# Copying the gather indices once per window of eight chunks, in a graph attention kernel

## The chip, the cores and the metric

The kernel runs on one core of a Trainium2 chip. The metric is the device time of one execution in microseconds; of several executions the median is given.

## What is computed

The reference is a pre-norm residual layer around one graph attention layer, with N = 6250 nodes, D = 256 features and E = 200000 edges. The edges are sorted by their destination node `dst`; the sources `src` are random. Cut to what matters:

```python
h = relu(layernorm(x))
q, k, v = h @ wq + bq, h @ wk + bk, h @ wv + bv
scores = sum(q[dst] * k[src], -1) * D ** -0.5 + (edge_weight * we + be)
exp_s = exp(scores - segment_max(scores, dst)[dst])
attn = exp_s / max(segment_sum(exp_s, dst)[dst], 1e-12)
out = segment_sum(v[src] * attn[:, None], dst)
y = layer_norm(h + out + h @ ws + bs, g1, b1)
z = layer_norm(y + gelu(y @ w_ff1 + b_ff1) @ w_ff2 + b_ff2, g2, b2)
return x + z
```

The destinations are drawn as N times the square of a uniform number, so low node numbers have more edges than high ones.

## The kernel before

The program has three blocks, one after the other. The first makes h for 49 blocks of 128 nodes, stores h in HBM (`h_rows`), folds the query and key weights into one projection that is kept in SBUF in three bf16 parts (`q3`), and prepares tables. The second, the edge block, goes over all edges. The third divides the sums by the weights, applies the value projection, and does the feed forward part and both norms.

The edge block, on which the change bears, cuts the sorted edges into **chunks** of 512 edges (C = 512, J = 4 columns of 128). There are 391 chunks, padded to TP = 392. G = 8 chunks make a **window** (line 25 gives G, and NW = 49 windows). A **step** is one pair of a chunk and a block of 128 destination nodes: a chunk whose edges cross from one node block into the next takes two steps, which is why there are more steps than chunks. A table, `steps_tab`, gives each step its chunk and block. The engines do the following:

- **POOL** (line 776 on, helper `gather`) fetches the source rows. For each chunk it waits until the chunk's slot in `rows` is free (semaphore `slot_free`) and until the indices are there (`idx_set`). Then come four times an indirect DMA of 128 rows of 1 KB from `h_rows` (line 787), and behind each a copy of one column of indices from the large table `idx_all` to the small tile `idx` (line 789). That column belongs to the chunk four further on (LEAD = 4), so `idx` is a ring of eight chunks by four columns that is always filled half a ring ahead.
- **SP** (lines 753 to 771) waits, chunk by chunk in order, until the four gathers of the chunk have landed (line 756) and raises `chunk_landed` (line 757). Then it waits until the step that used a slot is summed and raises `slot_free`. A gather may be at most LEAD chunks ahead of the last landed one, and eight slots ahead of the last summed one. SP also loads the destinations, half a window at a time (line 770).
- **DVE** per step: the masked maximum (line 971), the dot products of query rows and gathered rows, four of them (line 914, which waits for `chunk_landed`), the sum with the edge term (line 920), the kept maximum (line 976), the one-hot mark of the destinations for a later step (line 903), and the addition into `acc` (line 931). At every eighth step it loads a new piece of the step table.
- **ACT** per step: two exponentials (lines 876 and 877), two copies from PSUM (line 880), and the mask (line 865).
- **PE** per step: transposes (lines 842 and 815), the expansion of the query rows by the one-hot matrix (line 809), and the weighted sum of the gathered rows (line 855).

The first 16 columns of `idx` are set by POOL in the first block (line 369), after `idx_all` is complete.

Of the kernel before, what the change touches and what calls it, by code (L numbers as in the profile page):

```python
# [7 lines left out]
I32 = mybir.dt.int32  # L8
# [5 lines left out]
P = 128  # L14
J = 4
# [4 lines left out]
G = 8  # L20
WC = G // 2
LEAD = 4
# [7 lines left out]
def ceil_div(a, b):  # L30
    return -(-a // b)


def gnn_layer(nc, x, src, dst, edge_weight, wq, bq, wk, bk, wv, bv, ws, bs, we, be, g1, b1, g2, b2,
              w_ff1, b_ff1, w_ff2, b_ff2, out):
    N, D = x.shape
# [7 lines left out]
    B = ceil_div(N, P)  # L44
    NB = B + 1
    T = ceil_div(E, C)
    TP = ceil_div(T, G) * G
    NW = TP // G
# [18 lines left out]
    with ctx:  # L67
        def sb(name, shape, dt=F32):
            return ctx.enter_context(nc.sbuf_tensor(name, shape, dt))

        def sem(name):
            return ctx.enter_context(nc.semaphore(name))

        def dram(name, shape, dt=F32):
            return nc.dram_tensor(name, shape, dt).ap()

        h_rows = dram("h_rows", (B * P, D))
# [26 lines left out]
        free_tab = sb("free_tab", [1, TP + LEAD], I32)  # L104
        idx_all = sb("idx_all", [P, R], I32)
        ew_all = sb("ew_all", [P, R + J])
        idx = sb("idx", [P, G * J], I32)
        dst_words = sb("dst_words", [P, G * C // 2], I32)
        dst_of = dst_words[:].bitcast(I16)
        w1_sb = dst_words[:, 0:DC * F].bitcast(F32).rearrange("p (c n) -> p c n", c=DC)  # L110
# [7 lines left out]
        def part(n, dt=F32):  # L118
            used[0] += n
            assert used[0] <= WORK, used  # L120
            a = work[:, used[0] - n:used[0]]
            return a if dt == F32 else a.bitcast(dt)
# [36 lines left out]
        def spare(n, dt=F32):  # L159
# [18 lines left out]
        at = B * WORDS_B - staged  # L178
# [24 lines left out]
        plan_consts, dst_cast, dst_out, falls_done, ends_compared, chunks_counted, steps_known, sums_known, marked, counts_ready, rows_copied, free_ready, plan_done = (  # L203
            sem(n) for n in ("plan_consts", "dst_cast", "dst_out", "falls_done", "ends_compared", "chunks_counted", "steps_known", "sums_known", "marked",
                             "counts_ready", "rows_copied", "free_ready", "plan_done"))
        plan = sem("plan")
        idx_set, dst_in = sem("idx_set"), sem("dst_in")
# [55 lines left out]
        with nc.Block() as block:  # L263
# [49 lines left out]
            @block.gpsimd  # L313
            def _(pool):
                g = nc.gpsimd
                pool.memset(ident[:], 0.0).then_inc(ident_set, 1)
                pool.wait_ge(ident_set, 1)
                pool.affine_select(out=ident[:], in_=ident[:], compare_op=ALU.not_equal, fill=1.0, base=0,
                                   pattern=[[-1, P]], channel_multiplier=1).then_inc(ident_set, 1)
                pool.iota(row_i, [[1, HEAD]], base=0, channel_multiplier=0)  # L320
                pool.iota(below_i, [[0, 1]], base=0, channel_multiplier=P)
                pool.iota(below_row_i, [[P, P]], base=0, channel_multiplier=0)
                pool.memset(tri, 1.0)
                pool.memset(is_block, 1.0)
                pool.iota(node_i, [[P, NB]], base=0, channel_multiplier=1).then_inc(consts, 1)
                pool.memset(q3[:, B], 0.0)

                pool.wait_ge(x_zero, 1)
                link = 0
                for n, row, parts in ((D, row_of["bs"], s_bias3), (D1, q_bias, q_bias3)):  # L330
                    if n == D:
                        pool.wait_ge(biases_in, 3 * 16)
                    else:
                        pool.wait_ge(wqk_copied, DC + 1)
                    hi, mid, rest = bias_hi[:, 0:n], bias_mid[:, 0:n], bias_rest[:, 0:n]
                    g.tensor_copy(hi, row).then_inc(bias_link, 1)
                    pool.wait_ge(bias_link, link + 1)
                    g.tensor_tensor(rest, row, hi, ALU.subtract).then_inc(bias_link, 1)
                    pool.wait_ge(bias_link, link + 2)
                    g.tensor_copy(mid, rest)  # L340
                    g.tensor_copy(parts[0:1, 0:n], hi[0:1, :]).then_inc(bias_link, 1)
                    pool.wait_ge(bias_link, link + 3)
                    g.tensor_copy(parts[32:33, 0:n], mid[32:33, :])
                    g.tensor_tensor(parts[64:65, 0:n], rest[64:65, :], mid[64:65, :], ALU.subtract).then_inc(bias_link, 1)
                    link += 4
                    pool.wait_ge(bias_link, link)
                g.tensor_copy(onesb_rows, ones[:]).then_inc(biases_split, 1)

                pool.wait_ge(consts, 1)
                g.tensor_copy(srow, row_i)  # L350
                g.tensor_copy(node[:], node_i)
                pool.affine_select(out=tri, in_=tri, compare_op=ALU.is_ge, fill=0.0, base=0, pattern=[[1, P]], channel_multiplier=-1)
                pool.affine_select(out=is_block, in_=is_block, compare_op=ALU.is_ge, fill=0.0, base=B - 1, pattern=[[0, 1]], channel_multiplier=-1)
                g.tensor_copy(below_row, below_row_i)
                pool.memset(pad_s, PAD_DST)
                pool.wait_ge(ends_in, 2 * TG * 16)
                g.tensor_copy(ends, ends_i)
                g.tensor_copy(firsts, firsts_i).then_inc(plan_consts, 1)
                pool.wait_ge(list_in, 3 * 16)
                g.tensor_copy(dst_s[0:EDGE_P, :], dst_a[0:EDGE_P, :]).then_inc(dst_cast, 1)  # L360
                pool.wait_ge(plan_consts, 1)
                g.tensor_scalar(firsts, firsts, -float(P), None, ALU.add).then_inc(plan_consts, 1)
                pool.wait_ge(plan_consts, 2)
                for k in range(TG):
                    g.tensor_scalar(chunk_below[:, k, :], below_row, ends[:, k:k + 1], None, ALU.is_gt)
                    last = g.tensor_scalar(chunk_begun[:, k, :], below_row, firsts[:, k:k + 1], None, ALU.is_gt)
                last.then_inc(ends_compared, 1)
                pool.wait_ge(tab_copied, 2)
                g.tensor_copy(idx[:, 0:LEAD * J], idx_all[:, 0:LEAD * J]).then_inc(idx_set, LEAD)

                def clear(first, end):
                    pool.wait_ge(h_done, min(end, B))
                    pool.memset(acc[:, first:end, :], 0.0)

                for k in range(4):
                    clear(k * XG, (k + 1) * XG)
                clear(FULL, NB)
# [312 lines left out]
        rows = part(S * J * D1).rearrange("p (u j n) -> p u j n", u=S, j=J)  # L690
# [13 lines left out]
        rows_in = [[sem(f"rows_in{u}_{j}") for j in range(J)] for u in range(S)]  # L704
        slot_free, chunk_landed = sem("slot_free"), sem("chunk_landed")
# [4 lines left out]
        with nc.Block() as block:  # L710
# [65 lines left out]
            @block.gpsimd  # L776
            def _(pool):
                n, m, rounds = counts(pool)

                def gather(first, u, next_first):  # L780
                    chunk = pool.to_reg(first + (u + 1))
                    pool.wait_ge(dst_out, 2 * 16)
                    pool.wait_ge(slot_free, chunk)
                    pool.wait_ge(dst_out, 2 * 16)
                    pool.wait_ge(idx_set, chunk)
                    for j in range(J):
                        pool.indirect_dma_start(rows[:, u, j, 0:D], None, h_rows, bass.IndirectOffsetOnAxis(idx[:, u * J + j:u * J + j + 1], 0)).then_inc(rows_in[u][j], 16)  # L787
                        at = (u + LEAD) % G * J + j
                        copied = nc.gpsimd.tensor_copy(idx[:, at:at + 1], idx_all[:, next_first(j)])  # L789
                    copied.then_inc(idx_set, 1)  # L790

                with pool.Fori(0, rounds) as r:
                    with pool.Fori(0, NW - 1) as i:
                        first = pool.snap(pool.to_reg(r * TP + i * G), min_val=0, max_val=B * TP)
                        for u in range(G):
                            gather(first, u, lambda j: bass.ds(i * (G * J) + ((u + LEAD) * J + j), 1))
                    first = pool.snap(pool.to_reg(r * TP + (NW - 1) * G), min_val=0, max_val=B * TP)
                    for u in range(G):
                        gather(first, u, lambda j: slice((((NW - 1) * G + u + LEAD) % TP) * J + j, (((NW - 1) * G + u + LEAD) % TP) * J + j + 1))

            @block.tensor
            def _(pe):
# [587 lines left out]
```

## Time and profile before

| | us |
|---|---|
| median of 3 runs | 2562.84 |
| lowest, highest | 2562.78, 2564.1 |
| profiled execution, own time | 2571.49 |
| profiled execution, span | 2569.4 |

| engine | busy us | share of the span |
|---|---|---|
| PE matmul | 2285.8 | 89% |
| PE weight load | 1811.4 | 70% |
| POOL | 1963.4 | 76% |
| DVE | 1757.6 | 68% |
| ACT | 1141.8 | 44% |

The gathers of the edge block start between 167.3 us and 2251.3 us of the span, so this block is four fifths of the program. The span runs from the first to the last instruction; the execution's own time also has what lies around that. Busy times of different engines overlap. "PEld" in a row is the weight load of PE. A row names the line of the source, the engine, the operation and the tiles it writes and reads; `work` is the large tile that holds `rows` and most of the working buffers, so a gather reads "work<-h_rows,idx". "idle before" is the time for which an engine stood still before an instruction, and the arrow names what ended it; "issue" means that no other engine or transfer did.

### The profile page before, as it was taken

Reading aid. Unit: us, or ns where it says so; the run is one execution under the profiler, and the core shown is the slowest. Engines: PE = TensorE matmul, PEld = TensorE weight load, DVE = VectorE, ACT = ScalarE, POOL = GpSimd, SP = SyncE. Lnnn points to the kernel's source line nnn. Section 1 sums busy time; section 2 is a strip of 40 time slices with the busy share of each in tenths; the row PEclk is TensorE's granted clock in tenths of the full one; section 3 lists DMA queues with packets and bytes.
Section 4 is the critical chain, followed back from the end, with each engine's and each line's share of the span. In section 5 each row is a group of like instructions: output and inputs, shape, how many; then the busy total and the mean of one; then the engine's idle time right before and its main releaser. Section 6 shows DMA issues by size and latency. Waiting matters only on the chain. (4 is left out here: it accounts for less than half of the span.)

```text
span 2569.4 us, 72091 instructions
## 1 busy us (share of the span) xinstructions
PE 2285.8 (89%) x14569; PEld 1811.4 (70%) x14570; DVE 1757.6 (68%) x7421; ACT 1141.8 (44%) x2765; POOL 1963.4 (76%) x3334
## 2 busy tenths in 40 slices
PE   5978888888888889889999999999999999989994
PEld 3756666666666667667677777777777777877883
DVE  5856666666666667667676777777777777775367
ACT  2544333434444444444444444444444444455454
POOL 2148888888888888888888888888888888802355
PEclk7989999999999999999999999999999999999997
DMA  6344444444444444444444444444444444440014
GB/s 201 109 132 123 123 123 122 123 124 123 123 124 123 123 123 124 125 125 124 124 123 124 122 123 124 122 123 124 122 123 124 123 122 123 123 106 29 0 53 138
DMA packets 140341, 302.96 MB, mean 118 GB/s; under 512 B 33710, under 2 KB 76833, under 8 KB 140312
## 3 DMA queue, kind: packets, MB, share of 16 engines
q0 software_dynamic: 75264, 205.62, 28.0%
q1 hardware_dynamic: 62910, 96.62, 11.2%
q10 hardware_dynamic: 2138, 0.40, 0.1%
q8 instruction: 10, 0.16, 0.0%
q14 instruction: 19, 0.16, 0.0%
HBM read 282.87 MB, written 19.65 MB: 118 GB/s over the span
## 5 line engine op out<-in xcount | busy, mean ns | idle before, releaser
L787 POOL DMA_INDIRECT work<-h_rows,idx x1568 | 1527.9, 974 | 252.2 <-issue 252.2
L855 PE MATMUL bank<-work 128*128 x3520 | 837.0, 380 | 0.0
L809 PE MATMUL bank<-q,onehot 128*128 x5304 | 745.4, 275 | 99.9 <-DVE work L914 90.0
L914 DVE SCALAR_TENSOR_TENSOR work<-bank,work 128x257 bf16<-128x257 f32 x1764 | 646.2, 424 | 255.1 <-SPq L757 250.6
L855 PEld LDWEIGHTS bank<-work 128*128 128x128 f32 x3520 | 635.1, 190 | 79.1
L809 PEld LDWEIGHTS bank<-q,onehot 128*128 128x128 bf16 x5304 | 501.4, 98 | 211.2 <-issue 145.3
L876 ACT ACTIVATE work<-work 128x1 f32<-128x1 f32 x440 | 129.6, 295 | 948.7 <-DVE work L971 948.7
L880 ACT COPY work<-bank 128x256 f32<-128x256 f32 x880 | 284.6, 375 | 234.6 <-PE bank L842 233.0
L842 PE MATMUL bank<-ident,work 128*128 128x128 f32 x1760 | 286.5, 285 | 76.9 <-ACT work L877 69.0
L903 DVE TENSOR_SCALAR onehot<-dst_words,node 128x512 bf16 x443 | 168.8, 381 | 263.0 <-issue 211.2
L842 PEld LDWEIGHTS bank<-ident,work 128*128 128x128 f32 x1760 | 184.6, 140 | 232.4 <-ACT work L877 225.3
L971 DVE CUSTOM_DVE_ANT_0 work<-bank,work 128x512 f32<-128x512 f32 x440 | 327.7, 745 | 22.7 <-issue 22.0
L789 POOL COPY idx<-idx_all 128x1 int32 (+1 forms) x1568 | 305.4, 195 | 10.6
L877 ACT ACTIVATE work<-work 128x512 f32<-128x512 f32 x440 | 310.7, 706 | 0.0
L815 PE MATMUL bank<-ident,work 128*128 128x128 f32 x1764 | 275.8, 279 | 26.2 <-DVE work L920 5.0
L865 ACT ACTIVATE work<-onehot 128x512 bf16<-128x512 bf16 x442 | 283.9, 642 | 1.6 <-DVE onehot L903 1.6
L815 PEld LDWEIGHTS bank<-ident,work 128*128 128x128 f32 x1764 | 193.6, 136 | 91.2 <-issue 75.4
L931 DVE SCALAR_TENSOR_TENSOR acc<-acc,work,bank 128x257 f32 x441 | 212.3, 481 | 26.2 <-issue 6.5
L914 DVE DVE_READ_ACCUMULATOR work<-bank,work 128x1 f32 x1764 | 145.1, 82 | 0.0
L920 DVE TENSOR_TENSOR work<-work,ew_all 128x4 f32<-128x4 f32 x441 | 72.3, 164 | 65.6 <-DVE work L914 11.8
L1166 POOL TENSOR_TENSOR work<-work 128x256 f32<-128x256 f32 x49 | 35.8, 730 | 90.2 <-DVE acc L1249 88.2
L1341 PE MATMUL bank<-work,dst_words 128*128 128x128 f32 x784 | 97.7, 278 | 2.7 <-DVE work L1243 2.6
(182 smaller groups left out, 1511.1 us busy)
## 6 DMA issues: line engine op xcount, KB each, us to landing
dst_words<-dst_short SPq DMA_DIRECT2D x99, 512.0 KB
work<-h_rows,idx POOLq DMA_INDIRECT x1568
h_rows<-work SPq DMA_DIRECT2D x49, 128.0 KB, 1.7
r_rows<-work SPq DMA_DIRECT2D x49, 128.0 KB, 1.7
work<-r_rows SPq DMA_DIRECT2D x49, 128.0 KB, 2.1
acc<-in_x SPq DMA_DIRECT2D x4, 1536.0 KB, 15.6
work<-in_x SPq DMA_DIRECT2D x48, 128.0 KB, 2.2
out<-work SPq DMA_DIRECT2D x48, 128.0 KB, 1.9
```

The source lines that it names most:

```text
L787: pool.indirect_dma_start(rows[:, u, j, 0:D], None, h_rows, bass.IndirectOffsetOnAxis(idx[:, u * J + j:u * J + j + 1], 0)).then_inc(rows_i ...
L789: copied = nc.gpsimd.tensor_copy(idx[:, at:at + 1], idx_all[:, next_first(j)])
L809: last = nc.tensor.matmul(banks[j][:, 0:D1], onehot[:, k, j, :], q3[:, bass.ds(b, 1), c, 0:D1], start=(c == 0), stop=(c == 2))
L815: last = nc.tensor.transpose(banks[4][:, j * P:(j + 1) * P], score[:, k, j:j + 1].broadcast_to([P, P]), ident[:])
L842: last = nc.tensor.transpose(banks[5 - half][:, j * P:(j + 1) * P], probsT[:, (2 * half + j) * P:(2 * half + j + 1) * P], ident[:])
L855: last = nc.tensor.matmul(banks[6 + k][:, 0:D1], probs[:, j, :], rows[:, bass.ds(slot, 1), j, :], start=(j == 2), stop=(j == 1))
L865: nc.scalar.activation(outside[:, k, :], onehot[:, k].rearrange("p j n -> p (j n)"), ACT.Copy, scale=BIG, bias=-BIG).then_inc(outside_done, 1)
L877: nc.scalar.activation(probsT, masked, ACT.Exp, bias=new_max, scale=-1.0).then_inc(exp_done, 1)
L880: nc.scalar.copy(probs[:, 2 * half:2 * half + 2, :].rearrange("p j n -> p (j n)"), banks[5 - half][:, 0:2 * P]).then_inc(probs_done, 1)
L914: last = nc.vector.scalar_tensor_tensor(out=product[:, j, 0:D1], in0=banks[j][:, 0:D1], scalar=SCALE, in1=rows[:, bass.ds(slot, 1), j, :], ...
L931: nc.vector.scalar_tensor_tensor(out=a, in0=a, scalar=decay[:, k:k + 1], in1=banks[6 + k][:, 0:D1], op0=ALU.mult, op1=ALU.add).then_inc(ad ...
L971: nc.vector.tensor_tensor_reduce(out=masked, in0=banks[4][:], in1=outside[:, k, :], scale=-1.0, scalar=old_max[:, k:k + 1], op0=ALU.add, o ...
```

## The change

The tile `idx` gets two halves of 32 columns, each of which holds the indices of a whole window. POOL no longer copies a column behind each gather. It issues the four gathers of a chunk one behind another, and behind the gathers of the seventh chunk of a window it copies all 32 columns of the next window into the other half with one instruction. The wait for `idx_set` stands once at the start of a window in place of once per chunk. The loop takes two windows per turn, and the last, 49th window stands behind it; after that, a last copy of the first window's columns waits until all chunks have landed. The copy in the first block sets 32 columns in place of 16. The other engines' programs are as before.

```diff
--- before.py
+++ after.py
@@ -104,7 +104,7 @@
         free_tab = sb("free_tab", [1, TP + LEAD], I32)
         idx_all = sb("idx_all", [P, R], I32)
         ew_all = sb("ew_all", [P, R + J])
-        idx = sb("idx", [P, G * J], I32)
+        idx = sb("idx", [P, 2, G * J], I32)
         dst_words = sb("dst_words", [P, G * C // 2], I32)
         dst_of = dst_words[:].bitcast(I16)
         w1_sb = dst_words[:, 0:DC * F].bitcast(F32).rearrange("p (c n) -> p c n", c=DC)
@@ -366,7 +366,7 @@
                     last = g.tensor_scalar(chunk_begun[:, k, :], below_row, firsts[:, k:k + 1], None, ALU.is_gt)
                 last.then_inc(ends_compared, 1)
                 pool.wait_ge(tab_copied, 2)
-                g.tensor_copy(idx[:, 0:LEAD * J], idx_all[:, 0:LEAD * J]).then_inc(idx_set, LEAD)
+                g.tensor_copy(idx[:, 0, :], idx_all[:, 0:G * J]).then_inc(idx_set, 1)
 
                 def clear(first, end):
                     pool.wait_ge(h_done, min(end, B))
@@ -777,26 +777,36 @@
             def _(pool):
                 n, m, rounds = counts(pool)
 
-                def gather(first, u, next_first):
+                def gather(first, half, u):
                     chunk = pool.to_reg(first + (u + 1))
                     pool.wait_ge(dst_out, 2 * 16)
                     pool.wait_ge(slot_free, chunk)
+                    for j in range(J):
+                        pool.indirect_dma_start(rows[:, u, j, 0:D], None, h_rows, bass.IndirectOffsetOnAxis(idx[:, half, u * J + j:u * J + j + 1], 0)).then_inc(rows_in[u][j], 16)
+
+                def next_idx(half, first):
+                    nc.gpsimd.tensor_copy(idx[:, half, :], idx_all[:, first]).then_inc(idx_set, 1)
+
+                with pool.Fori(0, rounds) as r:
+                    with pool.Fori(0, NW // 2) as i:
+                        for half in range(2):
+                            first = pool.snap(pool.to_reg(r * TP + i * (2 * G) + half * G), min_val=0, max_val=B * TP)
+                            ready = pool.to_reg(r * NW + i * 2 + (half + 1))
+                            pool.wait_ge(dst_out, 2 * 16)
+                            pool.wait_ge(idx_set, ready)
+                            for u in range(G):
+                                gather(first, half, u)
+                                if u == G - 2:
+                                    next_idx(1 - half, bass.ds(i * (2 * G * J) + (half + 1) * G * J, G * J))
+                    first = pool.snap(pool.to_reg(r * TP + (NW - 1) * G), min_val=0, max_val=B * TP)
+                    ready, all_landed = pool.to_reg(r * NW + NW), pool.to_reg(r * TP + TP)
                     pool.wait_ge(dst_out, 2 * 16)
-                    pool.wait_ge(idx_set, chunk)
-                    for j in range(J):
-                        pool.indirect_dma_start(rows[:, u, j, 0:D], None, h_rows, bass.IndirectOffsetOnAxis(idx[:, u * J + j:u * J + j + 1], 0)).then_inc(rows_in[u][j], 16)
-                        at = (u + LEAD) % G * J + j
-                        copied = nc.gpsimd.tensor_copy(idx[:, at:at + 1], idx_all[:, next_first(j)])
-                    copied.then_inc(idx_set, 1)
-
-                with pool.Fori(0, rounds) as r:
-                    with pool.Fori(0, NW - 1) as i:
-                        first = pool.snap(pool.to_reg(r * TP + i * G), min_val=0, max_val=B * TP)
-                        for u in range(G):
-                            gather(first, u, lambda j: bass.ds(i * (G * J) + ((u + LEAD) * J + j), 1))
-                    first = pool.snap(pool.to_reg(r * TP + (NW - 1) * G), min_val=0, max_val=B * TP)
+                    pool.wait_ge(idx_set, ready)
                     for u in range(G):
-                        gather(first, u, lambda j: slice((((NW - 1) * G + u + LEAD) % TP) * J + j, (((NW - 1) * G + u + LEAD) % TP) * J + j + 1))
+                        gather(first, 0, u)
+                    pool.wait_ge(dst_out, 2 * 16)
+                    pool.wait_ge(chunk_landed, all_landed)
+                    next_idx(0, slice(0, G * J))
 
             @block.tensor
             def _(pe):
```

On POOL, at the start of the edge block's loop, the rows before are as follows. A DMA is one gather (`work` holds `rows`), ISA is the computation of the copy's address, and the words in brackets are the semaphores waited for. This is one chunk and the start of the next:

```order
L787 DMA work<-h_rows,idx 128x256 [waits dst_out,idx_set,slot_free]
L789 ISA
L789 COPY idx<-idx_all 128x1
L787 DMA work<-h_rows,idx 128x256
L789 ISA
L789 COPY idx<-idx_all 128x1
L787 DMA work<-h_rows,idx 128x256
L789 ISA
L789 COPY idx<-idx_all 128x1
L787 DMA work<-h_rows,idx 128x256
L789 ISA
L789 COPY idx<-idx_all 128x1
```

Each gather is followed by an address computation and a copy of one column. With the change the seventh and eighth chunk of a window and the start of the next window read:

```order
L785 DMA work<-h_rows,idx 128x256 [waits slot_free,dst_out]
L785 DMA work<-h_rows,idx 128x256 x3
L788 ISA
L788 COPY idx<-idx_all 128x32
L781 REGISTER_ALU
L785 DMA work<-h_rows,idx 128x256 [waits slot_free,dst_out]
L785 DMA work<-h_rows,idx 128x256 x3
L793 ISA
L781 REGISTER_ALU [waits idx_set,dst_out]
L785 DMA work<-h_rows,idx 128x256 [waits slot_free,dst_out]
L785 DMA work<-h_rows,idx 128x256 x3
```

The gathers of a chunk now stand next to each other, and one copy of 32 columns stands between the seventh and the eighth chunk, with four gathers between it and the wait for `idx_set`.

## Rows read from the trace of the kernel before

**Rows 1.** The page: busy times, and groups by line (busy, mean ns | idle before, releaser).

```profile
PE 2285.8 (89%) x14569; PEld 1811.4 (70%) x14570; DVE 1757.6 (68%) x7421; ACT 1141.8 (44%) x2765; POOL 1963.4 (76%) x3334
...
L787 POOL DMA_INDIRECT work<-h_rows,idx x1568 | 1527.9, 974 | 252.2 <-issue 252.2
...
L789 POOL COPY idx<-idx_all 128x1 int32 (+1 forms) x1568 | 305.4, 195 | 10.6
```

**Rows 2.** Timeline of POOL in the middle of the edge block (start us, us, what).

```profile
999.98 0.98 POOL L787 DMA_INDIRECT work<-h_rows,idx  x1 [0.15 <-issue]
1000.96 0.19 POOL L789 COPY idx<-idx_all 128x1 int32 x1
1001.31 0.97 POOL L787 DMA_INDIRECT work<-h_rows,idx  x1 [0.15 <-issue]
```

**Rows 3.** Who waited for whom, 160 to 2272 us (total us, times, longest).

```profile
POOL work L787 <- issue: 252.2, 1568, 10.8
DVE work L914 <- SPq L757: 250.6, 223, 10.7
...
PEld bank L842 <- ACT work L877: 225.3, 419, 2.3
```

**Rows 4.** Tile idx: durations in ns (min/median/max), first and last start in us.

```profile
L787 POOL DMA_INDIRECT work<-h_rows,idx x1568: 968/975/1182, 167.3 to 2251.3; - x196
L789 POOL COPY idx<-idx_all x1568: 189/193/292, 168.5 to 2252.2; 128x1 int32 x192, 128x1 int32<-128x1 int32 x4
L369 POOL COPY idx<-idx_all x1: 197/197/197, 68.6 to 68.6; 128x16 int32<-128x16 int32 x1
```

**Rows 5.** Line 971, once per step, and line 757, once per landed chunk.

```profile
L971 DVE CUSTOM_DVE_ANT_0 work<-bank,work x440: 736/745/752, 183.6 to 2265.0; 128x512 f32<-128x512 f32 x147
...
L757 SPq EVENT_SEMAPHORE  x392: 27/28/28, 178.7 to 2256.8; - x196
```

**Rows 6.** Timeline of DVE around two steps (a step starts with L971).

```profile
1007.60 0.74 DVE L971 CUSTOM_DVE_ANT_0 work<-bank,work 128x512 f32<-128x512 f32 x1
...
1009.93 0.43 DVE L914 SCALAR_TENSOR_TENSOR work<-bank,work 128x257 bf16<-128x257 f32 x1 [1.57 <-SPq L757]
...
1013.18 0.74 DVE L971 CUSTOM_DVE_ANT_0 work<-bank,work 128x512 f32<-128x512 f32 x1
```

**Rows 7.** Line 876, once per step, in six stretches (160, 300, 600, 900, 1200, 1500 us on).

```profile
L876 ACT ACTIVATE work<-work x23: 294/294/296, 184.4 to 295.9; 128x1 f32<-128x1 f32 x23
L876 ACT ACTIVATE work<-work x58: 294/294/297, 301.2 to 599.6; 128x1 f32<-128x1 f32 x58
L876 ACT ACTIVATE work<-work x60: 294/294/297, 604.3 to 896.8; 128x1 f32<-128x1 f32 x60
L876 ACT ACTIVATE work<-work x63: 294/294/297, 901.9 to 1199.7; 128x1 f32<-128x1 f32 x63
L876 ACT ACTIVATE work<-work x64: 294/294/296, 1205.2 to 1497.6; 128x1 f32<-128x1 f32 x64
L876 ACT ACTIVATE work<-work x66: 294/294/297, 1503.1 to 1795.5; 128x1 f32<-128x1 f32 x66
```

**Rows 8.** Line 787, four times per chunk, from 300 and from 600 us on.

```profile
L787 POOL DMA_INDIRECT work<-h_rows,idx x227: 968/975/1060, 299.3 to 599.8; - x114
L787 POOL DMA_INDIRECT work<-h_rows,idx x226: 968/975/984, 599.8 to 898.9; - x113
```

**Rows 9.** Timeline of POOL in the last window, whose copies have constant addresses.

```profile
2245.59 0.19 POOL L789 COPY idx<-idx_all 128x1 int32<-128x1 int32 x1
2245.94 0.97 POOL L787 DMA_INDIRECT work<-h_rows,idx  x1 [0.15 <-issue]
```

**Rows 10.** Stretches: engines' busy us, granted clock, share of the DMA engines, GB/s.

```profile
300.00:600.00 300.00, 259.65 (x1608) 191.80 (x1605) 190.39 (x860) 119.16 (x287) 263.67 (x453) 1.00 0.41 123
...
1800.00:2100.00 300.00, 283.22 (x1886) 229.58 (x1884) 223.16 (x1009) 139.58 (x335) 263.60 (x452) 1.00 0.41 123
```

## The prediction

> **What bounds the kernel now.** I read the busy times first. PE is the busiest engine with 89%, POOL has 76% and DVE 68% [rows 1]. By shares alone PE would be the bound and POOL would have a quarter of its time to spare. The waits say otherwise. Of POOL's idle time, 252.2 us stand before gathers, 1568 times, and all of it is put down to issue, none to a semaphore [rows 1]. The longest is the 10.8 us before the first gather [rows 3]. So in the edge block POOL never once waited for a free slot or for indices. The timeline shows what it does: a gather of 0.98 us, a copy of 0.19 us that starts as the gather ends, a gap of 0.15 us, and the next gather; from start to start 1001.31 - 999.98 = 1.33 us [rows 2]. 1568 gathers at 1.33 us are 2085 us, which is just the distance from the first gather at 167.3 to the end of the last copy at 2252.4 [rows 4]. POOL is a metronome of 4 x 1.33 = 5.32 us per chunk.
>
> The other side of that is on DVE: it waited 223 times, 250.6 us in all, for line 757, SP's message that a chunk has landed [rows 3]. So the gathers set the pace, and DVE, PE and ACT follow.
>
> How fast could the followers go? Line 971 runs once per step, 440 times, first at 183.6 and last at 2265.0 us [rows 5]. Of the 250.6 us of waits, 10.7 us lie before the first step [rows 3]. The 439 steps between take 2081.4 us, of which 239.9 us are waits for landed chunks, and that leaves (2081.4 - 239.9) / 439 = 4.19 us for a step that never waits. One step shows it: from 1007.60 to 1013.18 are 5.58 us with a wait of 1.57 us inside, so 4.01 us without it [rows 6]; the mean is higher since the steps at which the table is loaded are longer. The 4.19 us are a closed round: PE's transposes wait for ACT (225.3 us for line 877 in all [rows 3]), ACT for DVE, and DVE issues its own work nearly without a break.
>
> A chunk costs POOL 5.32 us and the followers 4.19 us times its number of steps. From 300 to 600 us there are 58 steps [rows 7] on 227/4 = 56.75 chunks [rows 8], nearly one each; from 1500 to 1800 us there are 66 on 56.5. So the slack of the followers is large at first and small later, but POOL has the longer time in all stretches.
>
> **What the change does, part by part.** *Removed:* 1568 copies, 305.4 us of POOL's busy time [rows 1], all of it on the path, since POOL never waits. *Added:* 49 copies of 32 columns. A copy of one column has a median of 193 ns and the copy of 16 columns took 197 ns [rows 4], so the time hardly depends on the number of columns; I take 0.20 us, with the gap of 0.15 us [rows 2] 0.35 us each, 17 us in all or 0.04 us per chunk. *Moved:* the wait for the indices stands once per window. The copy that it waits for is issued before the four gathers of the eighth chunk, about 4 us of POOL's work, so it is done when the wait comes. The last copy waits for the last chunk to land, behind all gathers; nothing is queued behind it on POOL in this block, and the followers have steps left then. The first block's copy grows from 16 to 32 columns, and after it POOL has long pauses: nothing. SP, DVE, ACT and PE have the same instructions.
>
> **The unknown** is the distance between two gathers that follow each other directly; no row of before shows such a pair. From below: the gather's own length, 0.975 us [rows 4], with no gap, or less if two could overlap. From above: 1.33 us, if the copy lay in time that the gather needs anyway. Between them lies 1.33 - 0.19 = 1.14 us, the distance with the copy's shown length taken out and the gap kept [rows 2]. I take 1.10 us, a little less than that: the shown 0.19 us is the same for one and for 16 columns, so it is nearly all fixed cost, and a copy should have some fixed cost outside its shown length as well. Per chunk that gives 4 x 1.10 + 0.04 = 4.44 us in place of 5.32.
>
> The Trainium skill, in Perfetto Trace Analysis, section GPSIMD Engine Instruction, says that an instruction there which reads no tensor reports no start, and that such work should be timed from start to start; its section on the software DMA path puts gathers in that class. The trace agrees in so far as the gap of 0.15 us is the same before each gather. By this rule 0.975 and 0.15 are only a split made by the reader of the trace, while 1.33 and the copy's 0.19 are real, and the sum with 1.14 us would be the better one: 4.60 us per chunk, 36 us of remainder by the sum below, 2359 us.
>
> **The sum.** If the gathers were never late, DVE's waits would vanish: the 239.9 us inside the block, say 240. That is the ceiling. What remains is where a chunk's 4.44 us are still longer than its steps. From the first landed chunk at 178.7 us [rows 5] to 300 us, 121.3 / 5.32 = 23 chunks land and 23 steps are made [rows 7]: 23 x (4.44 - 4.19) = 6 us. From 300 to 600 us: 56.75 x 4.44 = 252 us against 58 x 4.19 = 243 us, 9 us. From 600 to 900 us: 56.5 x 4.44 = 251 us against 60 x 4.19 = 251 us, nothing. Later there are 63, 64 and 66 steps on 56.5 chunks, so the followers are the bound, and POOL begins to wait for `slot_free`. Remainder 15 us, gain 240 - 15 = 225 us. From the profiled execution's 2571.5 us that gives 2346 us, and from the median of the runs, 8.7 us lower than it, 2562.8 - 225 = **2338 us**. So 305 us of copies bring 225 us, because the followers' 4.19 us come next.
>
> **Rivals.** *A, the followers bound everywhere.* If gathers follow at 1.04 us or less, a chunk costs at most 4.20 us, the remainder is nothing, and the time is 2562.8 - 240 = 2322 us. For it: the gap of 0.15 us might belong to the change from copy to gather. The Trainium skill, in Perfetto Trace Analysis, section DMA Instruction — SWDGE (GPSIMD), says that two of the engine's processors make the descriptors and that each goes on by itself. By that, one could begin the next gather while the other ends the last; that the copy starts with no gap behind the gather agrees. Against it: the gap stands before gathers, and a gather still stands behind a gather.
>
> *B, part of the copy was hidden.* The gather may end later than shown and the copy may have lain over this end; then the gap grows. Halfway, at 1.215 us, a chunk costs 4.90 us and the remainders are 16, 35, 26, 13, 10 and 0 us in the six stretches (23 chunks, then 56.75, 56.5, 56.5, 56.75, 56.5, against the steps of [rows 7]), 100 in all; gain 140 us, 2423 us. Fully hidden, at 1.33 us, POOL's pace would not change, and the 17 us of the new copies would be offset by nothing: about 2563 to 2580 us.
>
> *C, the change does not do what it says,* because POOL's sequencer and not its processors set 1.33 us: then the copies were free. Against it: in the last window the copies have constant addresses, so that the sequencer has less to do there, and the gap is the same 0.15 us [rows 9]. Same time, 2563 us.
>
> *D, slower.* Gathers without a pause between them could each take longer, because their descriptors are written faster than the rings are emptied, or because DVE holds the memory port. It decides from a gather of more than 1.33 us: at 1.40 us a chunk costs 5.64 us, 392 x 0.32 = 125 us more, 2688 us. Against it: the DMA engines are busy to 0.41 [rows 10], and at 4.44 us per chunk that would be 0.41 x 5.32 / 4.44 = 0.49; all 1568 gathers took 968 to 1182 ns beside a DVE that was busy two thirds of the time [rows 4, 10]. The Trainium skill warns in SBUF — State Buffer, under Who interferes with whom, that DVE in some modes keeps this engine from writing descriptors. The narrow spread of the gathers says that this does not happen here.
>
> **How the numbers follow.** The forecast, gathers at 1.06 to 1.15 us apart, has 0.60; A 0.22; B with a gap in between 0.09; fully hidden or C 0.05; D 0.04. The forecast's band is 2325 to 2364 us (4.28 and 4.64 us per chunk, remainders of 2 and 41 us). Below it, A gives 2322 us, and if a step without waits were 0.02 us shorter than the mean, 440 x 0.02 = 9 us less, 2313 us. Above it, B reaches 2423 us at halfway; the range takes in most of that and leaves out C and D. Range **2312 to 2412 us**. What a measurement of this kernel can tell from no change is 0.2%, about 5 us. Faster by more: forecast, A and B, 0.91; within: 0.05; slower: 0.04.
>
> **What would show it.** POOL's timeline would have gathers 1.10 us apart, and one copy of about 0.2 us in 32 gathers. DVE's wait for line 757 would fall from 250.6 to about 25 us, nearly all of it in the first 600 us; from about 900 us on gathers at the start of a chunk would wait for SP's `slot_free`, which no gather does now. PE would be above 95% busy in the edge block, and the last step near 2265 - 225 = 2040 us. The time before 167 us and the third block would be unchanged. It would be wrong if two neighbouring gathers lay more than 1.2 us apart, if their own length rose, or if the step without waits grew above 4.19 us when nothing slows it.

## The result and the profile after

The changed kernel takes 2459.6 us (median of 4 runs, 2456.57 to 2460.01), the kernel before 2563.47 us beside it. The ratio is 0.9587, with a 95% interval of 0.9569 to 0.9604: 104 us faster. The forecast was 225 us faster, 2338 us, with a range of 2312 to 2412 us. The sign was right and the size was twice too large, outside the range. In one later session every kernel, the one before included, took some 3320 to 3340 us, and its totals are compared only with each other.

The page of the changed kernel shows the groups that answer to [rows 1]:

```profile
span 2458.0 us, 68766 instructions
...
PE 2246.5 (91%) x14569; PEld 1819.7 (74%) x14570; DVE 1759.9 (72%) x7421; ACT 1141.8 (46%) x2765; POOL 1625.4 (66%) x1815
...
L785 POOL DMA_INDIRECT work<-h_rows,idx x1568 | 1485.7, 948 | 481.5 <-issue 464.5
```

POOL's busy time fell by 338 us: the 305 us of old copies went, 11 us of new ones came, and the gathers, shown as 948 in place of 974 ns, are 42 us shorter in all. But the idle time before gathers rose from 252 to 482 us, and 464.5 us of it are still put down to issue. Another 9.1 us in 30 gaps are put down to SP's line 761, which raises `slot_free`, but none of these gaps is longer than 0.3 us, like all others: no other engine holds POOL up. The timeline of POOL shows where it went; it answers to [rows 2]:

```profile
1000.09 0.95 POOL L785 DMA_INDIRECT work<-h_rows,idx  x1 [0.30 <-issue]
1001.35 0.94 POOL L785 DMA_INDIRECT work<-h_rows,idx  x1 [0.31 <-issue]
1002.59 0.95 POOL L785 DMA_INDIRECT work<-h_rows,idx  x1 [0.30 <-issue]
1003.53 0.23 POOL L788 COPY idx<-idx_all 128x32 int32 x1
1003.92 0.97 POOL L785 DMA_INDIRECT work<-h_rows,idx  x1 [0.16 <-POOL idx L788]
1005.20 0.95 POOL L785 DMA_INDIRECT work<-h_rows,idx  x1 [0.31 <-issue]
1006.45 0.94 POOL L785 DMA_INDIRECT work<-h_rows,idx  x1 [0.30 <-issue]
```

Two gathers with nothing between them are 1.25 us apart, not 1.10. The gap before a gather is 0.30 us when a gather stands ahead of it and 0.16 us when a copy does. Where the one copy of a window stands, the distance is 1003.92 - 1002.59 = 1.33 us, just what it was behind every gather before. So a copy of one column took 0.19 us in the trace and 0.08 us out of POOL's round. The copy of 32 columns costs a little more: the gather behind it is shown 0.03 us longer, and the next one starts 1005.20 - 1003.92 = 1.28 us after it, so both distances together are 1.33 + 1.28 - 2 x 1.25 = 0.11 us longer than without a copy. The medians over all 48 such places say the same.

The waits, as in [rows 3]:

```profile
POOL work L785 <- issue: 464.5, 1490, 11.0
...
DVE work L924 <- SPq L757: 135.7, 156, 10.2
```

DVE's wait for landed chunks fell by 115 us, from 250.6 to 135.7, and did not vanish. Line 971 is now line 981:

```profile
L981 DVE CUSTOM_DVE_ANT_0 work<-bank,work x440: 736/745/753, 181.3 to 2151.3; 128x512 f32<-128x512 f32 x147
```

The 439 steps take 1970.0 us where [rows 5] has 2081.4. Without the waits inside, 135.7 - 10.2 = 125.5 us, a step takes 1844.5 / 439 = 4.20 us, against 4.19 before. All of the gain is in this stretch: 111.4 us of the 111.4 us between the spans of the two profiled executions (the medians differ by 104 us, since the profiled execution of before was 8 us above its median), the time ahead of it being 2.3 us shorter (181.3 against 183.6) and the time behind it 2.3 us longer (306.7 against 304.4).

### The profile page after: what moved, and what is told of

Same layout as the page of the kernel before. It is cut to its first block and busy times, and to the rows that moved or that the text cites. A ratio compares the mean times of both kernels' runs of the same rounds, so it can differ in the third digit from the quotient of the medians.

```text
span 2458.0 us, 68766 instructions
## 1 busy us (share of the span) xinstructions
PE 2246.5 (91%) x14569; PEld 1819.7 (74%) x14570; DVE 1759.9 (72%) x7421; ACT 1141.8 (46%) x2765; POOL 1625.4 (66%) x1815
## 5 line engine op out<-in xcount | busy, mean ns | idle before, releaser
L785 POOL DMA_INDIRECT work<-h_rows,idx x1568 | 1485.7, 948 | 481.5 <-issue 464.5
L924 DVE SCALAR_TENSOR_TENSOR work<-bank,work 128x257 bf16<-128x257 f32 x1764 | 646.5, 425 | 142.0 <-SPq L757 135.7
L819 PEld LDWEIGHTS bank<-q,onehot 128*128 128x128 bf16 x5304 | 508.8, 98 | 132.4 <-issue 68.7
L930 DVE TENSOR_TENSOR work<-work,ew_all 128x4 f32<-128x4 f32 x441 | 72.6, 165 | 65.6 <-DVE work L924 11.7
L1112 ACT ACTIVATE work<-bank,bff_col 128x128 f32<-128x128 f32 x196 | 56.0, 370 | 100.2 <-PE bank L1351 100.2
L1351 PEld LDWEIGHTS bank<-work,dst_words 128*128 128x128 f32 x784 | 93.5, 195 | 4.5 <-issue 2.8
```

The costliest lines, as they stand in the source:

```text
L819: last = nc.tensor.matmul(banks[j][:, 0:D1], onehot[:, k, j, :], q3[:, bass.ds(b, 1), c, 0:D1], start=(c == 0), stop=(c == 2))
L924: last = nc.vector.scalar_tensor_tensor(out=product[:, j, 0:D1], in0=banks[j][:, 0:D1], scalar=SCALE, in1=rows[:, bass.ds(slot, 1), j, :], ...
L1351: last = nc.tensor.matmul(banks[2 + at % 2][:, m * P:(m + 1) * P], w1_sb[:, c, m * P:(m + 1) * P], unit_T[:, at % 2, c * P:(c + 1) * P], s ...
```

## The experiments

Two theories stood at the outset on why a copy costs less than it lasts. **H**: a gather has a hidden tail of 0.30 us after its shown end, and one copy fits beside it. **P**: a copy holds POOL for some 0.08 us only, and the rest of its 0.19 us is latency that lies beside the next instruction. Rivals were that the sequencer sets the pace (**S**), and that the waits and not the copies were what the change removed (**W**).

**One copy per chunk.** The kernel before, with one part of the change alone:

```diff
                     for j in range(J):
                         pool.indirect_dma_start(...)
-                        at = (u + LEAD) % G * J + j
-                        copied = nc.gpsimd.tensor_copy(idx[:, at:at + 1], idx_all[:, next_first(j)])
-                    copied.then_inc(idx_set, 1)
+                    at = (u + LEAD) % G * J
+                    nc.gpsimd.tensor_copy(idx[:, at:at + J], idx_all[:, next_first]).then_inc(idx_set, 1)
```

> The kernel before with one copy of four columns behind the fourth gather of each chunk, in place of four copies of one column; the ring of eight chunks and the wait for idx_set in every chunk stay. Theory H and theory P (both: what a copy takes from POOL's round is 0.08 us, and 1.25 us is the gather's own round): three neighbouring gathers 1.25 us apart and one 1.33 us, so 4 x 1.25 + 0.08 = 5.08 us per chunk, and about 10 us above the changed kernel, 2470 us. Rival W (the changed kernel gains because the wait for the indices stands once per window and not once per chunk): the chunk's first gather comes late here, and the time stays within 20 us of the kernel before.

Measured: 2483.03 us, 23 us above the changed kernel's 2459.6, ratio to the kernel before 0.9679 (0.9663 to 0.9695). POOL's timeline shows one chunk:

```profile
1001.09 0.97 POOL L787 DMA_INDIRECT work<-h_rows,idx  x1 [0.16 <-issue]
1002.37 0.95 POOL L787 DMA_INDIRECT work<-h_rows,idx  x1 [0.30 <-issue]
1003.62 0.95 POOL L787 DMA_INDIRECT work<-h_rows,idx  x1 [0.30 <-issue]
1004.87 0.95 POOL L787 DMA_INDIRECT work<-h_rows,idx  x1 [0.30 <-issue]
1005.82 0.19 POOL L789 COPY idx<-idx_all 128x4 int32 x1
1006.17 0.97 POOL L787 DMA_INDIRECT work<-h_rows,idx  x1 [0.16 <-issue]
```

A chunk takes 1006.17 - 1001.09 = 5.08 us, as both theories had it. The wait for `idx_set` stands in each chunk here, and still three quarters of the gain are there: W falls. The 10 us that I expected between this kernel and the changed one were too few: with the changed kernel's 4 x 1.25 + 0.11 / 8 = 5.01 us per chunk, 392 x 0.07 = 27 us are due where POOL is the bound throughout.

**Two and four copies behind each gather.** The kernel before with one, and with three, further copies of a column into spare tiles:

```diff
                         at = (u + LEAD) % G * J + j
+                        for extra in range(1):
+                            nc.gpsimd.tensor_copy(spare_idx[:, extra, at:at + 1], idx_all[:, at:at + 1])
                         copied = nc.gpsimd.tensor_copy(idx[:, at:at + 1], idx_all[:, next_first(j)])
```

> The kernel before with a second copy of one column (constant address, into a spare tile) behind each gather. Theory H (the gather has a hidden tail of about 0.30 us, and a copy takes its full 0.19 us, of which all but 0.08 us lay beside that tail): the second copy finds the tail used up and costs 0.19 us or more, gathers 1.52 us or more apart, 2860 us or more. Theory P (a copy occupies the engine for only 0.08 us, the rest of its 0.19 us is latency beside the next instruction): gathers 1.41 us apart, 2563 + 1568 x 0.08 = 2690 us. Theory S (the sequencer sets 1.25 us and each instruction in its stream adds its issue of about 0.05 us): 1.38 us apart, about 2640 us.

> The kernel before with three more copies of one column (constant address, spare tiles) behind each gather. Theory H: 1.33 + 3 x 0.19 = 1.90 us or more between gathers, 3455 us or more. Theory P: 1.33 + 3 x 0.08 = 1.57 us, 2940 us. Theory S: 1.33 + 3 x 0.05 = 1.48 us, 2800 us.

Measured: 2744.64 and 3106.75 us, one run each. The timelines of POOL with two copies, and with four:

```profile
1001.42 0.97 POOL L788 DMA_INDIRECT work<-h_rows,idx  x1 [0.15 <-issue]
1002.40 0.19 POOL L791 COPY work<-idx_all 128x1 int32<-128x1 int32 x1
1002.53 0.17 POOL L792 COPY idx<-idx_all 128x1 int32 x1
1002.86 0.97 POOL L788 DMA_INDIRECT work<-h_rows,idx  x1 [0.15 <-issue]
```

```profile
1000.57 0.97 POOL L788 DMA_INDIRECT work<-h_rows,idx  x1 [0.15 <-issue]
1001.55 0.42 POOL L791 COPY work<-idx_all 128x1 int32<-128x1 int32 x3
1001.91 0.17 POOL L792 COPY idx<-idx_all 128x1 int32 x1
1002.24 0.97 POOL L788 DMA_INDIRECT work<-h_rows,idx  x1 [0.15 <-issue]
```

Gathers are 1.44 and 1.67 us apart. By the times, (2744.64 - 2564.47) / 1568 = 0.115 us for the second copy, and (3106.75 - 2744.64) / 3136 = 0.115 us for each of the next two. The second copy starts 0.13 us after the first and ends after it: two copies overlap by a third of their length. H wanted 0.19 us or more for each further copy and falls. P's number, 0.08 us, was too low for the further ones, but its kind is right: a copy costs POOL less than the trace shows, 0.08 us behind a gather and 0.115 us behind another copy. S wanted 0.05 us and did not get it. As to where the copy's other 0.11 us go, these numbers give a split: 0.19 - 0.115 = 0.075 us are not paid behind a copy either, so they lie beside whatever comes next, and only 0.035 us more are saved behind a gather. What is peculiar to the gather, such as a hidden tail, explains no more than these 0.035 us.

**Gathers of half, and of a quarter, of the rows.** The changed kernel, with 64 rows and later with 32; the other rows hold ones, so part of the data is missing:

```diff
-pool.indirect_dma_start(rows[:, u, j, 0:D], None, h_rows, bass.IndirectOffsetOnAxis(idx[:, half, ...], 0))
+pool.indirect_dma_start(rows[0:64, u, j, 0:D], None, h_rows, bass.IndirectOffsetOnAxis(idx[0:64, half, ...], 0))
```

> The changed kernel with gathers of 64 rows in place of 128, on partitions 0 to 63; the other 64 rows of every gather are left out and hold ones. If a gather's round is made by its rows, it falls to about 0.63 us, POOL is far faster than the others, and the time shows the followers' floor: 440 steps of 4.19 us, 2322 us, with DVE's wait for line 757 near nothing. If it is a fixed cost per instruction, it stays near 1.25 us and 2460 us. In between, by the split.

> The changed kernel with gathers of 32 rows; the other 96 rows of every gather are left out and hold ones. From 1.25 us at 128 rows and 1.207 us at 64 rows the line gives 0.67 ns per row and 1.164 us fixed. If it is a line: 1.186 us from start to start at 32 rows, 4.74 + 0.02 us per chunk, and about 2390 us. If the cost goes by groups of rows, another distance.

The half took 2405.3 us. The first rows are of its timeline, the last ones of the quarter's:

```profile
1005.30 0.90 POOL L785 DMA_INDIRECT work<-h_rows,idx  x1 [0.31 <-issue]
1006.51 0.90 POOL L785 DMA_INDIRECT work<-h_rows,idx  x1 [0.30 <-issue]
```

```profile
1006.04 0.87 POOL L785 DMA_INDIRECT work<-h_rows,idx  x1 [0.30 <-issue]
1007.21 0.87 POOL L785 DMA_INDIRECT work<-h_rows,idx  x1 [0.30 <-issue]
1008.39 0.87 POOL L785 DMA_INDIRECT work<-h_rows,idx  x1 [0.30 <-issue]
```

From start to start it is 1.25 us at 128 rows, 1.21 at 64 and 1.17 at 32 (expected 1.186). Gathers of a quarter of the rows take 6% less time. Carried on to no rows at all, that leaves some 1.15 us of a gather fixed, an estimate from these three distances. The quarter's total, 3338.77 us, says nothing here, since it comes from the later session; the distance between gathers of 128 rows was 1.25 us there too.

**Half the bytes.** The changed kernel with rows of 512 bytes, the other half of each row left out:

```diff
-pool.indirect_dma_start(rows[:, u, j, 0:D], None, h_rows, bass.IndirectOffsetOnAxis(...))
+pool.indirect_dma_start(rows[:, u, j, 0:P], None, h_rows.rearrange("r (a n) -> (r a) n", a=2), bass.IndirectOffsetOnAxis(...))
```

> The changed kernel with gathers of 128 rows of 512 bytes in place of 1 KB (they read other data, and the second half of every row holds ones). In the run with half the rows a gather still took 1.21 us from start to start. Theory F (nearly all of a gather's round is a fixed cost of the instruction on POOL, whatever it moves): 1.25 us, 2460 us. Rival M (the transfer of 128 KB or its descriptors' sizes hold the next gather back): the distance falls clearly below 1.2 us and the time below 2400 us.

Measured: 2458.23 us, and the distance is 1.25 us as before:

```profile
1000.75 0.94 POOL L785 DMA_INDIRECT work<-h_rows,idx  x1 [0.30 <-issue]
1001.99 0.94 POOL L785 DMA_INDIRECT work<-h_rows,idx  x1 [0.30 <-issue]
1003.24 0.94 POOL L785 DMA_INDIRECT work<-h_rows,idx  x1 [0.30 <-issue]
```

The number of bytes has no part in it, and theory F, a fixed cost of the instruction on POOL, stands.

**Register moves ahead of each gather.**

```diff
                     for j in range(J):
+                        for extra in range(4):
+                            pool.reg_mov(scratch, extra + 1)
                         pool.indirect_dma_start(...)
```

> The changed kernel with four register moves in POOL's program ahead of every gather. The gathers of the changed kernel are 1.25 us apart, also where a register operation and two waits stand at the start of a chunk. Theory F (POOL's processors set the 1.25 us, the sequencer has time to spare): 1.25 us still, 2460 us. Rival S (the sequencer sets the distance): each move adds some 0.05 us, so 1.45 us apart and about 2460 + 1568 x 0.2 = 2770 us.

Measured: 2458.54 us, and gathers stay 1.25 us apart. But this run tests nothing. Its trace holds 68766 instructions, exactly as many as that of the changed kernel, where 6272 more were due. Line 788, where the moves stand, shows only the wait for the slot, once per chunk, although register moves of other lines do appear in these traces:

```profile
L788 POOLq EVENT_SEMAPHORE  x392: 17/17/17, 165.1 to 2116.1; - x196
```

The moves set a register that nothing reads, and they most likely never became part of the program. What settles S stands in the trace of the changed kernel. Ahead of each chunk's first gather the sequencer computes the chunk's number, in line 781; `POOLq` is POOL's sequencer:

```profile
L781 POOLq ALU_OP  x392: 32/32/49, 164.6 to 2113.0; - x196
L785 POOL DMA_INDIRECT work<-h_rows,idx x1568: 942/946/1257, 165.6 to 2132.0; - x196
```

The sequencer does this for the last chunk at 2113.0 us, and the first gather of that chunk starts at 2128.2 us. From the third chunk on it is 5.1 to 15.4 us ahead of the gathers at every chunk. This step stands behind the four gathers of the chunk before, so these had already left the sequencer; from the second chunk on that was so before the first of the four started. The sequencer also has more to do between two chunks than within one, yet the median distance is 1.25 us in both places. POOL's gathers do not wait for the sequencer, so S falls; "issue" in these rows is a gap that POOL makes itself.

**One gather per chunk.** The changed kernel with `for j in range(1)` in `gather` and in SP's wait; three of four gathered columns are left out.

> The changed kernel with only the first of a chunk's four gathers; the other three columns of rows are left out and hold ones. POOL needs 1.25 us per chunk and is no bound. It measures the floor of the other engines: if the 4.19 us of a step without waits are right and stay when nothing is late, 440 steps give 2322 us (the ceiling of the prediction's gain, 240 us), and gathers wait for slot_free. Rival: the 4.19 us hide waits that are put down to others, and the time falls to 440 x 4.0 us, 2240 us, or the engines hold each other up and it stays above 2340 us.

Measured: 2334.71 us. Who waited for whom, and line 982, once per step:

```profile
POOL work L785 <- SPq L761: 1425.0, 382, 8.3
```

```profile
L982 DVE CUSTOM_DVE_ANT_0 work<-bank,work x440: 734/745/753, 180.0 to 2028.0; 128x512 f32<-128x512 f32 x147
```

Now it is POOL that waits, for `slot_free`, and DVE has no wait for line 757 among its groups. A step takes (2028.0 - 180.0) / 439 = 4.21 us with everything there in time. The 4.19 us read from before by taking the waits away were right to 0.5%.

**SP fetches the indices, and five gathers are left away.** POOL has no copies at all; SP brings 32 columns by a transfer within SBUF at the end of each window, and the last window leaves out the five gathers of padding:

```diff
+                    idx_there = sp.to_reg(trip * 16 + 16)
+                    sp.dma_start(idx[:, half, :], idx_all[:, bass.ds(after_next * (G * J), G * J)]).then_inc(idx_in, 16)
+                    sp.wait_ge(dst_out, 2 * 16)
+                    sp.wait_ge(idx_in, idx_there)
+                    sp.sem_inc(idx_set, 1)
...
-                                if u == G - 2:
-                                    next_idx(1 - half, ...)
...
-                        gather(first, 0, u)
+                        gather(first, 0, u, LAST[u])
```

> The changed kernel with POOL left to gathers alone: SP loads the next window's 32 index columns by a transfer within SBUF after the last chunk of a window has landed, and the five gathers that would fetch only padding (the last one of chunk 390 and all of chunk 391) are left away, since no weight reaches these rows. If a gather is a fixed 1.25 us and POOL the bound to the end, the 49 copies' 0.08 us each give 4 us and the five gathers 6 us: about 2450 us. Rival: SP's wait for its own transfer at the end of each window holds back chunk_landed and costs more than it brings.

Measured: 2456.79 us, ratio 0.9567 (0.9554 to 0.9581). That is 2.8 us below the changed kernel, with intervals that overlap. The gathers behave as expected (1563 of them, the first and last start):

```profile
L799 POOL DMA_INDIRECT work<-h_rows,idx x1563: 942/946/1246, 168.6 to 2123.3; - x196
```

In the changed kernel they start from 165.6 to 2132.0 us, so they now take 11.7 us less; five gathers of 1.25 us and 49 copies of 0.11 us are 11.6 us. From the first gather to the last step, though, it is 184.7 to 2149.6 us for the steps here, against 181.3 to 2151.3: 4.7 us less counted from each one's first gather. The other engines are some steps behind when the gathers end. SP's wait for its own transfer did no visible harm.

To tell the 2.8 us apart, the changed kernel and this one were run side by side again.

> The changed kernel unaltered, beside the next one on the same chip, to compare the two closely: 2460 us.

> The kernel with SP loading the indices and five gathers fewer, unaltered. In the first look its gathers took 11.7 us less from first to last than the changed kernel's, but its last step came only 4.7 us earlier counted from its first gather. Theory: that is the effect, since the other engines are still behind by some steps when the gathers end and then set the end by themselves: about 5 us below the changed kernel, 2455 us. Rival: the first median, 2456.8 against 2459.6 us, was noise and they are equal to 0.1%.

Beside them the kernel before took 3333.48 us instead of 2564. There the changed kernel took 3323.95 us, ratio 0.9978 (0.9957 to 0.9998), and the version with SP 3319.97 us, 0.9965 (0.9939 to 0.9990). They don't settle whether the two differ. But they show the change from another side. The waits of the changed kernel there, 300 to 2900 us:

```profile
POOL work L785 <- SPq L761: 854.1, 300, 11.3
...
ACT work L890 <- remote: 584.3, 195, 5.0
DVE work L981 <- remote: 482.1, 89, 7.1
```

ACT and DVE stood still for up to 7 us at a time on something that the trace does not name ("remote"), and POOL waited for slots, 854 us in these 2600. The mean granted clock of TensorE was 0.897 of full speed, where it was 0.982 in the changed kernel's first profile. What held the engines up is open. The gathers themselves kept their median of 946 ns. With the other engines later, the gathers no longer set the pace, and 1519 copies fewer are worth 0.2%.

## Why the prediction was wrong, and where it was right

**What bounds the kernel** was right: POOL, though PE had the largest share. The changed kernel shows it, and so does the run with one gather per chunk, in which 229 us went away (2563.5 to 2334.7).

**The step that failed is "The unknown"**, the distance between two gathers that follow each other directly. I took 1.10 us, from 1.33 us less the copy's shown 0.19 us and a little more. It is 1.25 us. The bounds held, from 0.975 to 1.33 us, but I went to the wrong side of 1.14 us. The argument was that a copy should have some cost outside its shown length. The runs show the reverse: it has less cost than its length. Taking it away was charged with 1.33 - 1.10 = 0.23 us per gather and brought 0.08 us, since the gap ahead of a gather, which the prediction kept at 0.15 us, grew to 0.30 us. The 305.4 us of POOL's busy time that I called "all of it on the path" were 1568 x 0.08 = 125 us there. Two neighbouring gathers more than 1.2 us apart were among the signs of being wrong that the prediction named.

**The sum** holds once its input is mended. With 5.01 us per chunk the remainders are 23 x 0.82 = 19, 284 - 243 = 41, 283 - 251 = 32, 283 - 264 = 19, 284 - 268 = 16 and 283 - 277 = 6 us, 133 in all; 240 - 133 = 107 us of gain, 2456 us, where 2459.6 were measured. It holds by stretches too. DVE's waits for landed chunks in the changed kernel, without the one ahead of the first step, are 14, 41, 31, 22, 11 and 5 us in the same six stretches, and 1.4 us after them; from 300 to 600 us:

```profile
DVE work L924 <- SPq L757: 41.0, 47, 1.6
```

With the 4.85 us per chunk of the gathers of 64 rows (4 x 1.21 + 0.01) the same sum gives 87 us of remainder and 2410 us, measured 2405. The ceiling, rival A, was put at 2322 us; with one gather per chunk it was 2335.

**What would show it**: the gap was the wrong one, as said. DVE's wait was to fall to 25 us and fell to 136. The last step was to be near 2040 us and stood at 2151.3. Gathers at the start of a chunk were to wait for `slot_free` from 900 us on. None was held up: 30 gaps over the whole block are put down to it, but they are no longer than the 0.30 us found everywhere, and POOL issued its gathers at its own pace to the last one. PE was to be above 95% busy; the stretches that answer to [rows 10] have 91% and 97%:

```profile
300.00:600.00 300.00, 272.01 (x1727) 207.42 (x1728) 205.38 (x924) 127.96 (x307) 228.16 (x247) 1.00 0.43 131
1800.00:2100.00 300.00, 290.04 (x1989) 243.67 (x1987) 235.12 (x1068) 147.31 (x354) 228.28 (x248) 1.00 0.43 131
```

The window's copy was right: a median of 219 ns for 32 columns where 200 were assumed, and 0.11 us out of the round where 0.35 were charged. The wait for `idx_set`, the last copy and the first block cost nothing, as said.

**The rivals.** *B* named what happened, part of the copy hidden, and the gap did grow. Its reason, a gather that ends later than shown, explains 0.035 of the hidden 0.11 us; the other 0.075 us stay hidden behind another copy as well, as the doubled copies show. It had a chance of 0.09, with 1.215 us as its example, and the range ended at 2412 us, below what even that gives (2423 us). That was too little: the gap of 0.15 us was read off a pair of copy and gather, and nothing in the trace said that it would stay. *C*, in which the sequencer sets the pace, is excluded by the sequencer's lead, not by the register moves. In the kernel before it computed the address of a copy 1.4 to 8.1 us, by the median 8.0 us, ahead of that copy:

```profile
L789 POOLq FUSED_REGOPS  x1536: 46/46/65, 167.1 to 2201.7; - x192
```

*D* did not come: gathers became shorter, 948 against 974 ns.

On the Trainium skill's rule in Perfetto Trace Analysis (GPSIMD Engine Instruction), to time such work from start to start: the trace agrees, and more strongly than I used it. Start to start, 1.33 against 1.25 us, is the copy's true cost. Subtracting one shown duration from a distance, as I did, is what that rule warns of. The prediction called the copy's 0.19 us real by this rule; the page makes no exception for such an instruction. Its section DMA Instruction — SWDGE (GPSIMD), in which two processors each go on by themselves, would have allowed gathers closer than their length; the measured 1.25 us, more than the shown 0.95, speak against any gain from that here.

## What to carry to other kernels

An engine that never waits sets the pace, whatever the shares of busy time say, and the waits of the others for it bound what a faster one can bring. Before an instruction's shown duration is counted as time saved on such an engine, ask for the distance between its neighbours with and without it; if the trace has no such pair, keep the whole span between "all of it" and "none of it" in the range. A doubled copy is a cheap way to measure what a copy costs, and it gave the price here within 0.04 us. When instructions are added as a probe, count them in the trace before reading the time: a probe that is not there costs nothing either.

## What the runs showed of the hardware

A gather of 128 rows on POOL takes 1.25 us from start to start, and nearly all of that is fixed: 1.21 us for 64 rows, 1.17 us for 32, and 1.25 us for rows of half the bytes. A gather's shown length and the gap before it change places with what stands ahead: 0.95 and 0.30 us behind a gather, 0.97 and 0.15 us behind a copy. What fills the fixed part, some 1.15 us by the estimate above, is open; it is neither the sequencer, which ran 5.1 to 15.4 us ahead, nor the number of bytes. Whether the 0.30 us belong to the gather that ends or to the one that starts is open too. A copy of one column costs 0.08 us behind a gather and 0.115 us behind another copy, and one of 32 columns costs 0.11 us behind a gather. These are distances from start to start; the copies themselves are shown with 0.19 and 0.22 us.
